# A graph layer and a gated expert network on one core: the last two gathered units are cut as 256 and 53 nodes instead of 128 and 181, and the work is listed in another order

## The chip, the core and the metric

The kernel runs on one core of one Trainium2 chip. The core's engines run beside each other and meet only at semaphores: TensorE (PE; its weight loads are shown as PEld), VectorE (DVE), ScalarE (ACT), GpSimd (POOL, which here does nothing but issue gathers) and SyncE (SP, which issues most other transfers). The metric is the device time of one execution in microseconds (us). Before the change it is 402.69 us, the median of three runs (402.5 to 402.74). All matrices are float32.

## The reference, cut to what matters

There are 3125 nodes of 256 features and 50000 edges sorted by destination.

```python
agg = jax.ops.segment_sum(features[edge_src] * edge_weight[:, None], edge_dst, num_segments=3125)
x = x + agg @ W.T + b                       # features = layernorm(x)
n = layernorm(x)
shared = mlp(n)                             # 256 -> 256 -> 128 -> 256, relu
experts = [mlp_e(n) for e in range(4)]      # 256 -> 128 -> 64 -> 256 each
gates = softmax(n @ gW + gb)                # the two best of four, weighed by softmax(top two)
x = x + shared + sum(weight_e * experts[e]) # over the two chosen
```

## The kernel before, in words

**First phase, to about 46 us.** x is loaded, normalised and multiplied by W; the products stand in SBUF (`xn_all`) and in a table in memory (`normalised_rows`). This phase isn't touched.

**Two ways to sum over edges.** Nodes 0 to 2228 are *gathered*: POOL fetches the source row of each edge by indirect DMA, 128 rows in a call and 12 calls in a batch. There are 24 batches, 0 to 23; the last has 6 calls. VectorE makes selection matrices (`selectors`, lines 1567 and 1571), TensorE multiplies them with the rows (`select_batch`, line 1154), ScalarE copies the result (`copy_windows`, line 950), and `merge` (line 1190) adds the windows of a unit up. Nodes 2229 to 3124 are *dense*: VectorE and ScalarE make one-hot matrices from edge records (`onehots`, line 1621; `low_halves`, lines 919 and 923), TensorE builds an adjacency matrix from them (`build_group`, line 1208) and multiplies it with `xn_all` (`multiply`, line 1221).

**Batches on a ring.** The rows of a batch lie in a ring of three. So before POOL fetches batch b it waits until TensorE has used batch b - 3 (line 828). Batches 0 to 2 fetch rows of x itself; their selection matrices also need the rows' statistics (`row_statistics`, lines 1518 and 1522, and `row_shifts`, line 1530).

**Units.** The nodes go through the second half (bias, residual, layer norm, gates and the expert network) as 14 units of at most two tiles of 128: G0 to G9 gathered, D0 to D3 dense. For a unit, TensorE turns the normalised rows (`turn`, line 1233), multiplies in three pieces (`layer1`, line 1253), then `layer2` (1262 and 1266), the turned gates (1275), their spread (1290) and `layer3` (1300 to 1303). ScalarE does the ReLUs (1007, 1017, 1020). VectorE does `add_bias` (1634), `residual` (1647 to 1655), `normalise` (1665), `gates` (1679), routing, `weigh` (1788) and `finish` (1796). One set of buffers serves all units, so a unit's step often waits for the unit before.

**What sets the order.** Each engine runs its list from front to back. `schedule()` makes the four lists at build time: it plays the steps with rough durations and picks by the ranks in `RANKS`, `BUILD_RANKS` and `MULT_RANKS`. `UNIT_ORDER` says in which order units open. Semaphores are waited for in the instructions themselves, so a wrong guess of `schedule()` costs a wait, in which everything behind in that engine's list stands still.

Lines that matter for what follows:

```python
# schedule(), the bias step of a unit, VectorE: for a dense unit nothing but the bias before it is asked for
("dve", "bias", 0.1 + 0.28 * T, lambda: needs(0.0 if u.kind == "D" else of("merge"), prior("bias", one)))
# add_bias, what is waited for on the chip
if q == 0:
    dve.wait_ge(s_linear, 16)
if unit.kind == "D" and unit.i == 0:
    dve.wait_ge(s_shifted, 16 * sum(stores_of(v) for v in DENSE))
# POOL, before the gathers of batch b
if b >= RING:
    pool.wait_ge(s_used[slot], b // RING)
```

`s_shifted` is counted up by the four transfers of `load_shifted` (line 762), which load x once more, laid out by the dense units' tiles. SyncE issues them behind the first edge records and the weights (lines 744 and 745).

## Time and profile before

| | |
|---|---|
| median of 3 runs | 402.69 us (402.5 to 402.74) |
| the profiled execution's own time | 399.85 us |
| its span, first to last instruction | 397.8 us |
| PE busy | 358.7 us (90%) |
| DVE busy | 278.8 us (70%) |
| ACT busy | 201.6 us (51%) |
| POOL busy | 281.3 us (71%) |
| gathers | 36 from x, 246 from the table |
| mean granted TensorE clock | 0.979 of full speed |

Times of instructions are counted from the span's start. A row of the timeline gives the start, how long the merged instructions took together, engine, line, operation, tiles written and read, and how many; in brackets stands how long the engine sat idle before it. A matmul in float32 appears as two passes (x24 for 12 matmuls). Waits are put down to whoever released them last.

### The profile page before, as it was taken

What the parts mean: (1) busy time and instruction counts of PE and PEld (TensorE: products, weight loads), DVE (VectorE), ACT (ScalarE), POOL (GpSimd) and SP (SyncE); (2) the same over time, 40 slices, a digit from 0 to 9 for tenths busy, and PEclk for the clock granted to TensorE, in tenths of its full rate; (3) what the DMA queues carried; (4) which work ended last, traced back from release to release, by engine and by line L of the source; (5) the groups of instructions that cost most, each with busy time, mean ns of one, the idle gap of its engine ahead of it and who ended that gap; (6) DMA issues with size and microseconds to landing.
All of it is one profiled execution on the core that took longest, in us unless ns stands there. A gap on an engine that the chain in (4) does not pass through costs nothing.

```text
span 397.8 us, 8069 instructions
## 1 busy us (share of the span) xinstructions
PE 358.7 (90%) x2327; PEld 283.6 (71%) x2327; DVE 278.8 (70%) x1199; ACT 201.6 (51%) x553; POOL 281.3 (71%) x294
## 2 busy tenths in 40 slices
PE   4997769969899998869999999999999999998884
PEld 3885557747687877557887877877788677766672
DVE  6698999597489999460299999770249853659671
ACT  2566797466059979300079798322019521134241
POOL 7777777777777778777777777777777777777000
PEclk9999599999999999989999999999999999999999
DMA  6999649844444463534333434343433344334000
GB/s 201 376 334 308 155 103 318 206 95 105 108 113 108 105 135 83 122 109 130 108 105 108 129 99 133 96 130 105 133 103 103 101 133 129 109 107 132 28 15 25
DMA packets 53586, 53.16 MB, mean 134 GB/s; under 512 B 32507, under 2 KB 43493, under 8 KB 53413
## 3 DMA queue, kind: packets, MB, share of 16 engines
q0 software_dynamic: 13536, 36.98, 32.1%
q1 hardware_dynamic: 35220, 10.53, 11.5%
q10 hardware_dynamic: 4784, 5.11, 3.6%
q8 instruction: 21, 0.34, 0.4%
q14 instruction: 25, 0.20, 0.2%
HBM read 46.11 MB, written 6.48 MB: 132 GB/s over the span
## 4 chain that ended last, share of the span: by engine, by line
PE 47%; SPq 30%; issue 10%; DVE 8%; DMA 2%; ACT 1%; DVEq 0%; ACTq 0%
SPq L740 23%; PE agg_ps L1221 14%; PE hid_ps L1253 10%; PE window_ps L1154 4%; PE tok_ps L1302 4%; SPq L735 4%; PE agg_ps L1190 3%; PE tok_ps L1300 2%; PE hid_ps L1266 2%; PE hid_ps L1262 2%; DVE high_node L1621 2%; SPq L734 2%; DVE gate_x L1679 1%; DMA x_sb<-in_x 1%; PE agg_ps L1208 1%
## 5 line engine op out<-in xcount | busy, mean ns | idle before, releaser
L833 POOL DMA_INDIRECT rows<-normalised_rows,src_all x246 | 243.3, 989 | 75.0 <-issue 75.0
L1221 PE MATMUL agg_ps<-xn_all,dense 128*128 128x256 f32 x350 | 84.3, 389 | 0.0
L1253 PE MATMUL hid_ps<-xt,pack 128*128 128x256 f32 (+2 forms) x336 | 70.9, 357 | 3.1 <-ACT xt L988 3.1
L1221 PEld LDWEIGHTS agg_ps<-xn_all,dense 128*128 128x128 f32 x350 | 65.3, 193 | 11.4 <-issue 3.1
L1253 PEld LDWEIGHTS hid_ps<-xt,pack 128*128 128x128 f32 x336 | 56.1, 190 | 13.7 <-issue 7.8
L919 ACT ACTIVATE low_1h<-iota,lo_f 128x128 f32<-128x128 f32 x182 | 57.6, 394 | 0.4 <-ACT xn_all L905 0.4
L1621 DVE TENSOR_SCALAR high_node<-iota,hi_f,own_w 128x125 f32<-128x125 f32 x182 | 49.8, 363 | 0.2
L1007 ACT ACTIVATE h<-hid_ps,pack 128x256 f32<-128x256 f32 (+2 forms) x84 | 32.7, 440 | 27.5 <-PE hid_ps L1253 27.3
L817 POOL DMA_INDIRECT rows<-in_x,src_first x36 | 35.6, 988 | 11.1 <-issue 10.4
L1679 DVE CUSTOM_DVE_ANT_0 gate_x<-xn,shared 128x256 f32<-128x256 f32 x100 | 41.7, 478 | 0.1
L950 ACT ACTIVATE windows<-window_ps 128x256 f32<-128x256 f32 (+1 forms) x24 | 9.1, 378 | 64.3 <-PE window_ps L1154 64.3
L1154 PE MATMUL window_ps<-rows,select 128*32 128x256 f32 x564 | 37.9, 398 | 1.5 <-DVE select L1571 1.5
L1567 DVE TENSOR_TENSOR select<-slots,rel 128x384 f32<-128x384 f32 (+1 forms) x24 | 13.1, 548 | 27.9 <-PE window_ps L1154 27.9
L1208 PE MATMUL build_ps<-high_node,low_1h 128*128 128x125 f32 x184 | 26.6, 290 | 6.7 <-ACT low_1h L923 3.5
L1208 PEld LDWEIGHTS build_ps<-high_node,low_1h 128*128 128x128 f32 x184 | 24.3, 202 | 9.9 <-issue 5.7
L923 ACT ACTIVATE low_1h<-low_1h 128x512 f32<-128x512 f32 (+1 forms) x46 | 28.8, 626 | 1.4
L1154 PEld LDWEIGHTS window_ps<-rows,select 128*32 128x32 f32 x564 | 16.7, 113 | 17.6 <-issue 7.0
L1302 PE MATMUL tok_ps<-pack,h 128*128 128x256 f32 (+1 forms) x100 | 25.7, 378 | 0.0
L1190 PE MATMUL agg_ps<-windows,place 128*128 128x256 f32 (+1 forms) x92 | 21.9, 382 | 0.3 <-ACT windows L960 0.3
L1302 PEld LDWEIGHTS tok_ps<-pack,h 128*128 128x128 f32 (+1 forms) x100 | 18.7, 187 | 3.1
L1796 DVE TENSOR_TENSOR y<-tok_ps,x 128x512 f32<-128x512 f32 (+1 forms) x14 | 8.8, 630 | 15.4 <-PE tok_ps L1303 15.3
L1190 PEld LDWEIGHTS agg_ps<-windows,place 128*128 128x128 f32 (+1 forms) x92 | 17.0, 190 | 2.9 <-issue 0.8
(171 smaller groups left out, 518.7 us busy)
## 6 DMA issues: line engine op xcount, KB each, us to landing
rows<-normalised_rows,src_all POOLq DMA_INDIRECT x246
x_sb<-in_x SPq DMA_DIRECT2D x6, 512.0 KB, 10.6
normalised_rows<-xn_all ACTq DMA_DIRECT2D x6, 512.0 KB
records<-in_rec SPq DMA_DIRECT2D x184, 1.5 KB, 1.9
out<-y SPq DMA_DIRECT2D x10, 256.0 KB
pack<-in_packed SPq DMA_DIRECT2D x1, 1540.5 KB, 9.5
dense<-in_x_cols ACTq DMA_DIRECT2D x3, 512.0 KB, 8.9
x_sb<-in_x SPq DMA_DIRECT2D x3, 256.0 KB, 10.7
```

Of the source, the lines that this page charges most:

```text
L740: sp.dma_start(records[:, bass.ds(t + (REC0[v] + t0 + k), 1), :].rearrange("p t c -> p (t c)"), rec[bass.ds(at, P), :]).then_inc(s_records ...
L817: pool.indirect_dma_start(rows[:, b * BATCH + pos, :], None, x[:, :], bass.IndirectOffsetOnAxis(ap=src_first[:, c:c + 1], axis=0)).then_in ...
L833: pool.indirect_dma_start(rows[:, b % RING * BATCH + pos, :], None, table[:, :], bass.IndirectOffsetOnAxis(ap=src_all[:, c:c + 1], axis=0) ...
L919: last = act.activation(low_1h[:, k % RING, j, :], iota[:, 0:P], ACT.Abs, scale=-1.0, bias=lo_f[:, at + j:at + j + 1])
L1154: last = pe.matmul(window_ps[SLOT * g:SLOT * (g + 1), 0:D], select[:, b % RING, j, :], rows[:, b % RING * BATCH + pos, :], start=(i == 0), ...
L1190: last = pe.matmul(sums_of(unit)[:, t * D:(t + 1) * D], place[0:full, b % KEEP, at:at + P], windows[0:full, b % KEEP, :], start=(b == batc ...
L1208: last = pe.matmul(built_in(k)[:, j * width:(j + 1) * width], low_1h[:, k % RING, j, :], high_node[:, k % RING, j, :], start=True, stop=True)
L1221: last = pe.matmul(dense_ps[0:r, t * D:(t + 1) * D], dense[:, h, t * P:t * P + r], xn_all[:, h, :], start=(h == 0 and t == 0), stop=(h == ...
L1253: last = pe.matmul(by_half(u.hid_ps[b % 2])[:, m % 2, 0:tok], w, u.xt[:, k, 0:tok], start=(k == 0), stop=(k == KD - 1))
L1302: pe.matmul(o, u.h2[:, 1 + k, c], ew3_sb[:, k, :], start=False, stop=False)
L1621: last = dve.tensor_scalar(high_node[:, r, j, :], iota[:, 0:HI * WIN], hi_f[:, at + j:at + j + 1], own_w[:, at + j:at + j + 1], ALU.is_equ ...
L1679: dve.tensor_tensor_reduce(out=gate_x[:, done % 2, :], in0=u.xn[:, t, :], in1=gate_w_sb[:, e, :], scale=1.0, scalar=gate_b_sb[:, e:e + 1], ...
```

## The change

Two things change. The last two gathered units are cut otherwise: G8 takes tiles 15 and 16 (256 nodes) and G9 only the 53 nodes of tile 17. G8's sums then need batches 19 to 22 and G9's need 22 and 23. Before, G8 needed 19 to 21, and G9, with 181 nodes, 21 to 23. And all lists are made anew with other ranks and another order of units: D0 opens ahead of G0, and D2 behind G6. No function changes.

```diff
-GATHERED += [Unit("G", 8, 15, 1, P, 15 * P), Unit("G", 9, 16, 2, P + HALF, 16 * P)]
+GATHERED += [Unit("G", 8, 15, 2, PAIR, 15 * P), Unit("G", 9, 17, 1, HALF, 17 * P)]
-UNIT_ORDER = "G0 D0 G1 G2 D1 G3 G4 G5 D2 G6 G7 G8 D3 G9"
+UNIT_ORDER = "D0 G0 G1 G2 D1 G3 G4 G5 G6 D2 G7 D3 G8 G9"
-RANKS = {"open": 3, "near": 0.07, "behind": 0.36, "dve_behind": 0.94, "act_behind": 0.23, "hurry": 1.58,
+RANKS = {"open": 3, "near": 0.06, "behind": 0.27, "dve_behind": 0.42, "act_behind": 0.23, "hurry": 1.58,
...
-MULT_RANKS = (1.55, 1.41, 10.13, 3.23)
+MULT_RANKS = (1.27, 1.41, 9.18, 3.23)
```

VectorE's list where the first phase ends. Line 1579 is the last step ahead of the lists, 1825 the branch into them, 1621 the one-hots of groups 2 and 3, 1587 and 1589 the first records of block 1. What an instruction waits for stands in brackets. Before:

```order
L1579 TENSOR_SCALAR place<-iota,posn 128x256 [waits s_posn]
L1825 TENSOR_LOAD flag
L1825 ISA x2
L1825 COMPARE_AND_BRANCH
L1621 TENSOR_SCALAR high_node<-iota,hi_f,own_w 128x125 [waits s_keys]
L1621 TENSOR_SCALAR high_node<-iota,hi_f,own_w 128x125 x3
L1621 TENSOR_SCALAR high_node<-iota,hi_f,own_w 128x125 [waits s_keys,s_built]
L1621 TENSOR_SCALAR high_node<-iota,hi_f,own_w 128x125 x3
L1587 TENSOR_SCALAR hi_i<-records 128x16 [waits s_records1]
```

The same place now:

```order
L1579 TENSOR_SCALAR place<-iota,posn 128x256 [waits s_posn]
L1825 TENSOR_LOAD flag
L1825 ISA x2
L1825 COMPARE_AND_BRANCH
L1634 TENSOR_TENSOR x_sb<-x_sb,shared 128x512 [waits s_shifted,s_x_turned,s_linear]
L1621 TENSOR_SCALAR high_node<-iota,hi_f,own_w 128x125 [waits s_keys]
L1621 TENSOR_SCALAR high_node<-iota,hi_f,own_w 128x125 x3
L1621 TENSOR_SCALAR high_node<-iota,hi_f,own_w 128x125 [waits s_keys,s_built]
L1621 TENSOR_SCALAR high_node<-iota,hi_f,own_w 128x125 x3
L1587 TENSOR_SCALAR hi_i<-records 128x16 [waits s_records1]
```

The bias of D0 (line 1634, 128x512) has moved from far behind to the head of the list.

VectorE from there to the selection matrices of batch 1 (1567 and 1571), before. 1518 and 1522 are the statistics of batch 1's rows:

```order
L1608 SCALAR_TENSOR_TENSOR own_w<-own_w,records 128x16
L1518 BN_STATS row_stats<-rows 128x6 x12
L1522 BN_AGGR row_mv<-row_stats 128x2 x12
L1621 TENSOR_SCALAR high_node<-iota,hi_f,own_w 128x125 x8
L1530 TENSOR_TENSOR row_w<-w_all,row_rstd 128x12
L1621 TENSOR_SCALAR high_node<-iota,hi_f,own_w 128x125 x4
L1567 TENSOR_TENSOR select<-slots,rel 128x384
L1571 TENSOR_TENSOR select<-select,row_w 128x384
```

Now:

```order
L1608 SCALAR_TENSOR_TENSOR own_w<-own_w,records 128x16
L1518 BN_STATS row_stats<-rows 128x6 x12
L1522 BN_AGGR row_mv<-row_stats 128x2 x12
L1621 TENSOR_SCALAR high_node<-iota,hi_f,own_w 128x125 x4
L1530 TENSOR_TENSOR row_w<-w_all,row_rstd 128x12
L1621 TENSOR_SCALAR high_node<-iota,hi_f,own_w 128x125 x4
L1567 TENSOR_TENSOR select<-slots,rel 128x384
L1571 TENSOR_TENSOR select<-select,row_w 128x384
```

One group of four one-hots has moved behind them.

TensorE's list around the last two batches (1154; x12 is batch 22, x6 is batch 23). Before, where 128x128 at line 1253 is D3 and the last three rows belong to D3 and G9:

```order
L1253 MATMUL hid_ps<-xt,pack 128x128 x4
L1154 MATMUL window_ps<-rows,select 32x256 x6
L1253 MATMUL hid_ps<-xt,pack 128x128 x4
L1190 MATMUL agg_ps<-windows,place 128x256 x4
L1253 MATMUL hid_ps<-xt,pack 128x128 x4
L1262 MATMUL hid_ps<-h,pack 128x128 x2
L1266 MATMUL hid_ps<-h,pack 64x128 x4
L1275 MATMUL mid_ps<-ident_b,parts 79x128
L1290 MATMUL tok_ps<-mix_t,owner 128x128 x2
L1233 MATMUL mid_ps<-ident,xn 128x128 x4
```

Now, where the x5 at line 1190 is the merge of G8, the x4 at line 1233 its turn, the 128x256 at line 1253 its first layer and the x2 at line 1190 the merge of G9:

```order
L1154 MATMUL window_ps<-rows,select 32x256 x12
L1253 MATMUL hid_ps<-xt,pack 128x128 x4
L1190 MATMUL agg_ps<-windows,place 128x256 x5
L1253 MATMUL hid_ps<-xt,pack 128x128 x4
L1262 MATMUL hid_ps<-h,pack 128x128 x2
L1266 MATMUL hid_ps<-h,pack 64x128 x4
L1275 MATMUL mid_ps<-ident_b,parts 79x128
L1154 MATMUL window_ps<-rows,select 32x256 x6
L1290 MATMUL tok_ps<-mix_t,owner 128x128 x2
L1233 MATMUL mid_ps<-ident,xn 128x128 x4
```

A whole unit of 256 nodes (G8) now stands behind batch 22, with its turn behind batch 23, and the 53 nodes of G9 come last. GpSimd's list is the same.

## Rows read from the trace of the kernel before

**Rows 1.** The page: busy time and share of the span.

```profile
PE 358.7 (90%) x2327; PEld 283.6 (71%) x2327; DVE 278.8 (70%) x1199; ACT 201.6 (51%) x553; POOL 281.3 (71%) x294
```

**Rows 2.** What POOL waited for: engine, line, releaser, us, times, longest.

```profile
POOL rows L833 <- issue: 75.0, 246, 0.3
```

**Rows 3.** Timeline of POOL: first gathers of batches 3, 4; last of 22, 23.

```profile
50.13 0.95 POOL L833 DMA_INDIRECT rows<-normalised_rows,src_all  x1 [0.30 <-issue]
...
65.56 0.95 POOL L833 DMA_INDIRECT rows<-normalised_rows,src_all  x1 [0.30 <-issue]
...
359.32 1.15 POOL L833 DMA_INDIRECT rows<-normalised_rows,src_all  x1 [0.30 <-issue]
...
367.12 0.95 POOL L833 DMA_INDIRECT rows<-normalised_rows,src_all  x1 [0.30 <-issue]
```

**Rows 4.** Stretches: span, POOL busy, clock, DMA share, GB/s.

```profile
70.00:72.00 2.00, 1.54 (x2) 1.00 1.08 342
72.00:74.00 2.00, 1.55 (x2) 1.00 1.23 255
...
76.00:78.00 2.00, 1.41 (x2) 1.00 0.40 77
```

**Rows 5.** The four transfers of line 762: first and last start, time to landing.

```profile
L762 SPq DMA_DIRECT2D x_sb<-in_x x4: 434/570/679, 60.7 to 62.6; - x4
DMA to landing us min/median/max: 10.5/10.8/11.3
```

**Rows 6.** Timeline of VectorE after the first phase.

```profile
46.26 2.36 DVE L1621 TENSOR_SCALAR high_node<-iota,hi_f,own_w 128x125 f32<-128x125 f32 x8
...
56.51 1.10 DVE L1621 TENSOR_SCALAR high_node<-iota,hi_f,own_w 128x125 f32<-128x125 f32 x4
...
58.11 0.56 DVE L1571 TENSOR_TENSOR select<-select,row_w 128x384 f32<-128x384 f32 x1
...
87.02 0.68 DVE L1634 TENSOR_TENSOR x_sb<-x_sb,shared 128x512 f32<-128x512 f32 x1
```

**Rows 7.** TensorE: batches 0, 1, 22 (line 1154) and sixteen products (line 1221).

```profile
45.85 2.79 PE L1154 MATMUL window_ps<-rows,select 128*32 128x256 f32 x24 [1.50 <-DVE select L1571]
...
59.26 1.50 PE L1154 MATMUL window_ps<-rows,select 128*32 128x256 f32 x24
...
61.69 7.08 PE L1221 MATMUL agg_ps<-xn_all,dense 128*128 128x256 f32 x32
...
363.80 1.50 PE L1154 MATMUL window_ps<-rows,select 128*32 128x256 f32 x24
```

**Rows 8.** What ended VectorE's and TensorE's two longest waits near 170 us.

```profile
DVE hi_i L1587 <- DMA records<-in_rec: 8.7, 3, 4.8
...
PE tok_ps L1290 <- DVE mix_t L1781: 7.1, 5, 4.6
```

**Rows 9.** A stretch after the last gather: span, TensorE busy, clock, DMA share, GB/s.

```profile
370.00:371.00 1.00, 1.00 (x8) 1.00 0.00 0
```

**Rows 10.** TensorE and PEld near the end: G7, G8, D3, and the last output.

```profile
343.96 0.60 PE L1233 MATMUL mid_ps<-ident,xn 128*128 128x128 f32 x4
...
356.93 0.70 PE L1300 MATMUL tok_ps<-pack,h 128*128 128x256 f32 x2 [0.85 <-DVE h L1788]
...
359.74 0.27 PE L1303 MATMUL tok_ps<-b_parts,mix_t 79*128 79x256 bf16 x1
...
360.77 2.90 PEld L1253 LDWEIGHTS hid_ps<-xt,pack 128*128 128x128 f32 x24 [0.78 <-issue]
360.80 3.07 PE L1253 MATMUL hid_ps<-xt,pack 128*128 128x128 f32 x24 [0.57 <-ACT xt L988]
...
375.99 1.16 PE L1253 MATMUL hid_ps<-xt,pack 128*128 128x128 f32 x8
...
382.09 0.27 PE L1303 MATMUL tok_ps<-b_parts,mix_t 79*128 79x256 bf16 x1
...
393.44 0.69 DVE L1796 TENSOR_TENSOR y<-tok_ps,x 128x512 f32<-128x512 f32 x1 [3.32 <-PE tok_ps L1303]
```

More of the change, by code:

```diff
@@ L165 @@
 STATS_BEHIND = 3
-UNIT_ORDER = "G0 D0 G1 G2 D1 G3 G4 G5 D2 G6 G7 G8 D3 G9"
-RANKS = {"open": 3, "near": 0.07, "behind": 0.36, "dve_behind": 0.94, "act_behind": 0.23, "hurry": 1.58,
-         "batch": 0.99, "rawturn": 1.65, "rawlin": -10.68, "merge": 1.53, "windows": 4.07,
-         "built": 1.89, "rowstd": 2.86, "rawxt": 6.45, "rawout": -0.2, "low": 7.97, "select": -3.77,
-         "select_late": 8.67, "place": 7.59, "records": 6.65, "onehot": 0.5, "rowstats": 3.06,
-         "rowshifts": -1.63}
-BUILD_RANKS = (3.27, 4.1, 2.6, -3.72)
-MULT_RANKS = (1.55, 1.41, 10.13, 3.23)
+UNIT_ORDER = "D0 G0 G1 G2 D1 G3 G4 G5 G6 D2 G7 D3 G8 G9"
+RANKS = {"open": 3, "near": 0.06, "behind": 0.27, "dve_behind": 0.42, "act_behind": 0.23, "hurry": 1.58,
+         "batch": 0.99, "rawturn": 1.36, "rawlin": -10.4, "merge": 1.53, "windows": 4.07, "built": -3.9,
+         "rowstd": 2.86, "rawxt": 6.06, "rawout": 0.18, "low": 7.76, "select": -4.24,
+         "select_late": 7.28, "place": 5.89, "records": 3.37, "onehot": 0.5, "rowstats": 3.46,
+         "rowshifts": -2.1}
+BUILD_RANKS = (3.02, 4.36, 6.09, -3.72)
+MULT_RANKS = (1.27, 1.41, 9.18, 3.23)
 GATHER_US = 1.275
```

## The prediction

> **What bounds the kernel now.** I read the page first: TensorE is busy 90% of the span, everything else far less [rows 1]. That looks like a TensorE kernel, so the next view is the waits of POOL, the one engine with a fixed amount of work that nothing can hide: its 246 gathers from the table never waited for another engine, only for their own issue, 0.3 us each [rows 2]. Its timeline says what that means: from 50.13 to the last gather at 367.12 there are 246 gathers, so (367.12 - 50.13) / 245 = 1.29 us each, 15.5 us for a batch of 12, without a gap [rows 3]. The last nodes can't be summed before the last rows are there. The transfers end within the 2.9 us from 367.12 to 370.0 [rows 3, 9]; I take 2.7 us from issue to landing, so batch 22's rows land at 359.32 + 2.7 = 362.0 and batch 23's at 369.8. TensorE reaches batch 22 at 363.80 [rows 7], 1.8 us later. So POOL and TensorE are nearly even: a stop of POOL's stream lengthens the kernel by nearly its whole length, and a few us won on TensorE alone bring little.
>
> **Part one: D0's bias at the head of VectorE's list.** For the planner the step is free at once. On the chip it waits for `s_shifted`, four transfers that SyncE issues at 60.7 to 62.6 and that land 10.5 to 11.3 us later [rows 5], the last at 62.6 + 11.3 = 73.9. Before, the step stood at 87.02 and waited for nothing [rows 6]. VectorE begins its list at 46.26 [rows 6], so now it stands still there for some 25 us, and with it everything behind: the one-hots of groups 2 and 3 (TensorE's builds, and ScalarE's `low_halves` two groups later), the records, the statistics of batch 1's rows and batch 1's selection matrices. TensorE does its builds 0 and 1 and batch 0, and then waits as well.
>
> POOL isn't stopped at once. It fetches batch 3, and before batch 4 it needs batch 1 used. Before, TensorE began batch 1 at 59.26 [rows 7] and POOL went on at 65.56 [rows 3]: 6 us to spare, no more. The new time is a sum:
> - Landing. While the four transfers run, the DMA engines are full (shares 1.08 and 1.23 from 70 to 74, against 0.40 once only gathers are left) [rows 4]. POOL now falls silent after 66.8, which frees 0.4 of the engines for up to 9 us, 3.7 us of their time. I take 2.4 us off: 71.5. Bounds: 73.9 as traced, and 70 if all of it goes to these transfers.
> - The bias itself, 0.68 us [rows 6]: 72.2.
> - From the first one-hot to batch 1's selection matrices it took 58.11 + 0.56 - 46.26 = 12.4 us; one group of one-hots, 1.05 us, has moved behind: 11.3 us [rows 6]. Hence 83.5.
> - TensorE uses the first third of batch 1. At full clock that is 1.50 / 3 = 0.5 us, and after an idle time, as for batch 0, 2.79 / 3 = 0.9 us [rows 7]. With the semaphores 0.7 us: 84.2.
>
> POOL is held from 65.56 to 84.2: **18.6 us** (17 to 21 by the bounds).
>
> **Can it be held again, or catch up?** It can't catch up: the gathers have a fixed pace. Batch 5 needs batch 2 used. Behind batch 1's matrices VectorE now has five groups of one-hots (5.3), records and statistics (6.0: what 46.26 to 56.51 holds beside sixteen one-hots [rows 6]), a small block of records and three short steps (2.8): 14.1 us. TensorE has batch 1, 22 products of two passes at 7.08 / 32 = 0.22 us [rows 7], so 9.7, two builds and two steps on raw rows, about 14 us in all. POOL comes back to the ring after 15.5 + 0.7 us. That leaves about 2 us, so I count nothing, and up to 3 us for the range. Later batches have more room, since TensorE's lag is no larger than POOL's and shrinks: near 170 us it waited 4.6 us for VectorE, which itself stood 4.8 us on records from SyncE [rows 8]. SyncE's stream runs on by itself, so 18 us later these records are there (D3's last block, whose step has moved ahead of G1's `weigh`, would otherwise have cost some 10 us). The two waits are covered by the hold and bring nothing, because POOL sets the pace.
>
> **Part two: the cut of the last units.** Counted from batch 22's landing, the last output was made at 393.44 + 0.69 = 394.1, or 32.1 us [rows 10]. Now TensorE is there in time and waits for the rows. Behind batch 22 come D3's remaining layers and G8's merge, all done before batch 23's rows at 7.8 us, and batch 23 stands ahead of G8's turn: 7.8 + 1.5 + 0.3 = 9.6 us. For a unit of 256 nodes the trace has G7, from its turn at 343.96 to its third layer at 356.93, 13.0 us with batch 21 in it [rows 10]. G8 has no batch in it (-1.5), but G9's merge (+1.0), D3's third layer, half of it uncovered (+0.7), G9's turn and a third of its first layer (+1.2): 14.4 us, so G8's third layer begins at 24.0. It takes 359.74 + 0.27 - 356.93 = 3.1 us for two tiles [rows 10]: 27.1. G9's other two thirds of the first layer: 2.0, so 29.1. From there D3 needed 382.09 + 0.27 - (375.99 + 1.16) = 5.2 us to the end of its third layer [rows 10]; G9 has narrower ReLUs and no other unit between, 4.8: 33.9. Its output step, 0.5: 34.4 against 32.1. The stores took 397.8 - 394.1 = 3.7 us; two small ones, 3.5. In sum 34.4 + 3.5 - 32.1 - 3.7 = 2.1; I take **+2.0 us** (0 to +5): the 53 nodes are a unit of their own behind a full one, and the full one can't begin before batch 23.
>
> For the narrow passes I used the width of 128, since weight loads don't shrink: 24 loads take 2.90 us and the passes 3.07 us at 128 columns [rows 10], 121 ns a load. If the passes went by columns alone, the 16 behind G8 would take 16 x 53 ns = 0.9 us instead of 2.0, and the sum would be 1.1 us less. The Trainium skill, TensorE: Matmul & The Clock Gate, section on LDWEIGHTS, says that a load takes the time of its stationary columns over 1.2 GHz, whatever is moved past it. That would be an estimate of 107 ns for 128 columns, 1.7 us for the 16; it speaks against splitting off 53 nodes, and the row agrees in kind and is a little higher.
>
> **The sum.** 18.6 + 2.0 = 20.6 us on the profiled execution's 399.85 us (span 397.8): 420.5, span 418.4. The runs' median is 402.69, 2.84 above the profiled execution, so the measured time should be 402.69 + 20.6 = **423.3 us**, 5.1% slower. Not counted is the clock: it stood at half for batch 0, the engine's first work in the lists after an idle time, 2.79 us instead of 1.50 [rows 7]. Before batch 22 TensorE will idle again for some us, and could run the next few at half speed, 0 to 2 us more.
>
> **The rivals.**
> 1. *TensorE becomes the bound.* After the hold its whole backlog lies in front of it. By my count it reaches batch 22 some 3 us ahead of the rows; if the first part costs it 5 us more (half clock and sparse one-hots from 72 to 100), it comes 2 to 5 us late and everything ends there. For it: 90% busy. Against: it had idle time in the first 100 us which the hold swallows. 426 to 428 us. Chance 0.12.
> 2. *The ring jams again.* Batch 2 comes 3 us later than I think, POOL stands before batch 5 too, and the same before 6. For it: a margin of only 2 us. Price 3 to 8 us: 427 to 432. Chance 0.09.
> 3. *A shorter hold.* The transfers land at 67 to 69, since POOL is silent: the hold is 14 to 16 us, 418 to 421. Against: the engines are already full before POOL stops, and 10.5 us was the shortest landing. Chance 0.07.
> 4. *The other side: no hold, and the cut pays.* If the transfers were there when VectorE asks, POOL would never stop, and G9 with one tile could run right behind batch 23, in gaps that TensorE finds in G8. From batch 23's landing at 369.8: batch and merge 2, residual, norm and turn 4, first layer 3.1, ReLU 0.6, then 4.8 and 0.5: 15 us, so 384.8 instead of 394.1. It decides at a landing before 52 us, when the slack of 6 us would swallow the wait; the issue at 60.7 [rows 5] excludes that, unless the four aren't what the step waits for. 393 to 396 us. Chance 0.03; and 0.01 for nothing at all, at 402.7.
>
> **How the numbers follow.** My case has 0.68 and its own range is 420 to 427. Rivals 1 and 2 reach to 432, rival 3 to 418. With 2 in 10 left out: 418 to 430. This kernel can be told from no change at about 0.2%, 0.8 us; faster than that has 0.03, within it 0.01, slower 0.96.
>
> **What would show it right or wrong.** In the changed kernel's profile: line 1634, 128x512, as VectorE's first step after line 1579, at about 71.5 with some 25 us idle before it, released by a transfer; batch 1 at about 83.5; POOL's 13th table gather at about 84.2 with a wait of 18 to 19 us on TensorE, the only one of its kind; the last gather near 385.7; TensorE waiting for rows at batch 22 or 23; no long wait on records. The last output some 34 us after batch 22's rows. Wrong it is if VectorE doesn't wait there, if POOL is held under 14 or over 22 us, or if the end moves other than POOL's last gather by more than 5 us.

## The result, and the profile after

The changed kernel takes **424.54 us** (median of 4 runs, 423.46 to 424.84), the kernel before 402.72 on the same terms (4 runs, 402.5 to 403.1). The ratio is 1.055, with a 95% interval of 1.0508 to 1.0591: it is slower by about 22 us, where 423.3 was forecast. An execution now and then falls into a slower state; ratios leave such executions out, medians don't. The profiled execution took 424.84, its span is 422.8.

The page of the changed kernel: busy time, then three lines of the 40 slices (10.6 us each).

```profile
PE 362.3 (86%) x2327; PEld 288.0 (68%) x2327; DVE 278.7 (66%) x1199; ACT 203.5 (48%) x553; POOL 277.1 (66%) x294
...
PE   5996300699798789999999899999999999999985
...
POOL 7777771057777777777777777777777777773000
PEclk9997655699899988999999999999999999999997
```

The busy times are those of before within 5 us [rows 1]; the span grew by 25.0. So most of the added time is not work but idle time, and the slices show where: TensorE at 3, 0, 0 in slices 5 to 7, POOL at 1 and 0 in slices 7 and 8. The line of the clock falls with it.

Waits of POOL and TensorE in the changed kernel (engine, line, releaser, us, times, longest):

```profile
POOL rows L833 <- PE window_ps L1154: 21.8, 1, 21.8
```
```profile
PE build_ps L1208 <- DVE high_node L1621: 30.8, 3, 26.9
```

Before, POOL had no wait for TensorE [rows 2]. The releaser named is TensorE, which itself waited 26.9 us for VectorE. The chain is complete only with VectorE's timeline:

```profile
44.85 0.42 DVE L1579 TENSOR_SCALAR place<-iota,posn 128x256 f32<-128x256 f32 x1
72.87 0.69 DVE L1634 TENSOR_TENSOR x_sb<-x_sb,shared 128x512 f32<-128x512 f32 x1 [27.60 <-DMA x_sb<-in_x]
73.48 2.12 DVE L1621 TENSOR_SCALAR high_node<-iota,hi_f,own_w 128x125 f32<-128x125 f32 x8
...
84.12 0.56 DVE L1571 TENSOR_TENSOR select<-select,row_w 128x384 f32<-128x384 f32 x1
```

The bias of D0 is the first step of the list and waits 27.60 us for a transfer [rows 6 for its old place]. The four transfers and their landing:

```profile
L762 SPq DMA_DIRECT2D x_sb<-in_x x4: 434/510/924, 60.8 to 62.8; - x4
...
DMA to landing us min/median/max: 9.9/10.0/10.2
```

62.8 + 10.0 = 72.8: the landing is the end of the wait. (The times from issue to landing are 9.9 to 10.2 us; VectorE starts at 72.87.) Next TensorE, and then POOL, of the changed kernel:

```profile
44.98 2.79 PE L1154 MATMUL window_ps<-rows,select 128*32 128x256 f32 x24 [2.01 <-DVE select L1571]
74.64 2.07 PE L1208 MATMUL build_ps<-high_node,low_1h 128*128 128x125 f32 x8 [26.86 <-DVE high_node L1621]
...
82.57 2.07 PE L1208 MATMUL build_ps<-high_node,low_1h 128*128 128x125 f32 x8 [1.63 <-DVE high_node L1621]
84.44 1.71 PE L1208 MATMUL hid_ps<-high_node,low_1h 128*128 128x125 f32 x8
86.08 1.50 PE L1154 MATMUL window_ps<-rows,select 128*32 128x256 f32 x24
...
385.22 1.50 PE L1154 MATMUL window_ps<-rows,select 128*32 128x256 f32 x24
```
```profile
64.25 0.95 POOL L833 DMA_INDIRECT rows<-normalised_rows,src_all  x1 [0.30 <-issue]
87.02 0.95 POOL L833 DMA_INDIRECT rows<-normalised_rows,src_all  x1 [21.82 <-PE window_ps L1154]
...
377.03 0.95 POOL L833 DMA_INDIRECT rows<-normalised_rows,src_all  x1 [0.30 <-issue]
...
384.55 0.95 POOL L833 DMA_INDIRECT rows<-normalised_rows,src_all  x1 [0.30 <-issue]
```

Without the hold POOL's next gather would start at 64.25 + 0.95 + 0.30 = 65.50, as before at 65.56 [rows 3]. It starts at 87.02, 21.5 later. The last gather is only 17.4 later (384.55 against 367.12): the gathers won back 4 us. Batch 22 begins 21.4 later (385.22 against 363.80 [rows 7]).

Stretches of the changed kernel: from-to, length, busy time (instructions) of TensorE, PEld, DVE, ACT, POOL, then the granted clock, DMA share, GB/s.

```profile
44.00:100.00 56.00, 25.55 (x152) 20.68 (x152) 27.36 (x126) 23.53 (x63) 26.25 (x28) 0.69 0.47 123
100.00:385.20 285.20, 272.72 (x1809) 217.28 (x1808) 194.34 (x815) 143.15 (x390) 217.22 (x224) 0.98 0.42 113
385.20:419.00 33.80, 29.88 (x195) 21.73 (x194) 21.80 (x105) 12.04 (x41) 0.30 (x1) 0.97 0.09 28
...
350.00:380.00 30.00, 30.00 (x187) 23.16 (x186) 13.38 (x53) 8.73 (x23) 22.83 (x24) 1.00 0.40 116
...
416.00:420.00 4.00, 2.84 (x9) 1.13 (x8) 0.69 (x2) 0.19 (x1) 0.00 (x0) 0.61 0.03 8
```

And the same three stretches of the kernel before, up to its own batch 22 and its last output:

```profile
44.00:100.00 56.00, 46.79 (x338) 35.36 (x337) 48.02 (x213) 40.50 (x114) 43.15 (x43) 0.92 0.62 160
100.00:363.80 263.80, 252.43 (x1647) 201.19 (x1647) 176.69 (x740) 126.68 (x348) 201.39 (x205) 0.99 0.42 113
363.80:394.00 30.20, 24.46 (x173) 17.63 (x172) 19.23 (x93) 10.38 (x35) 3.35 (x4) 1.00 0.11 34
```

From 44 us to batch 22 TensorE has 298.3 us of work after and 299.2 before, the same. Its idle time grew from 20.6 to 42.9 us. The wait at the head is 26.9 of these, so the rest shrank by 4.6: that is all that TensorE made good. In the 30 us from 350 to 380 it is busy for all 30.00, and POOL gathers at its own pace. Batch 22's rows were there at 377.03 + 2.7 = 379.7, TensorE came at 385.22. The 2.7 us from issue to landing are the prediction's estimate; in experiment 6, where TensorE waits for batch 22's rows, it is 380.31 - 377.41 = 2.9. So the rows came 17.7 us later than before, TensorE 21.4, and TensorE set the end.

The last output and the stores of the changed kernel:

```profile
419.31 0.42 DVE L1796 TENSOR_TENSOR y<-tok_ps,x 128x256 f32<-128x256 f32 x1 [2.81 <-PE tok_ps L1303]
```

From batch 22's start to the end of that it is 419.73 - 385.22 = 34.5 us, against 394.13 - 363.80 = 30.3 before [rows 7, 10]. The span's sum: 21.4 (batch 22 begins later) + 4.2 (from there to the last output) - 0.6 (stores, 3.1 against 3.7) = 25.0.

### The profile page after: what moved, and what is told of

It is laid out like the page before. It is cut to its first block, busy times and chain, and to the rows that moved or that the text cites. A ratio compares the mean times of both kernels' runs of the same rounds, so it can differ in the third digit from the quotient of the medians.

```text
span 422.8 us, 8068 instructions
## 1 busy us (share of the span) xinstructions
PE 362.3 (86%) x2327; PEld 288.0 (68%) x2327; DVE 278.7 (66%) x1199; ACT 203.5 (48%) x553; POOL 277.1 (66%) x294
## 3 DMA queue, kind: packets, MB, share of 16 engines
q0 software_dynamic: 13536, 36.98, 30.3%
q1 hardware_dynamic: 35204, 10.53, 10.4%
## 4 chain that ended last, share of the span: by engine, by line
PE 63%; DVE 12%; SPq 12%; issue 5%; ACT 4%; DMA 2%; DVEq 0%
PE agg_ps L1221 18%; PE hid_ps L1253 12%; SPq L740 6%; PE window_ps L1154 6%; PE tok_ps L1302 6%; PE agg_ps L1190 4%; PE build_ps L1208 3%; PE tok_ps L1300 3%; PE hid_ps L1262 3%; PE hid_ps L1266 3%; DVE gate_x L1679 3%; DVE high_node L1621 2%; DMA x_sb<-in_x 2%; PE agg_ps L1208 2%; SPq L728 1%
## 5 line engine op out<-in xcount | busy, mean ns | idle before, releaser
L833 POOL DMA_INDIRECT rows<-normalised_rows,src_all x246 | 238.8, 971 | 96.5 <-issue 74.7
L1221 PE MATMUL agg_ps<-xn_all,dense 128*128 128x256 f32 x350 | 82.5, 382 | 0.9 <-ACT dense L969 0.9
L1253 PE MATMUL hid_ps<-xt,pack 128*128 128x256 f32 (+2 forms) x336 | 72.1, 359 | 1.0 <-ACT xt L988 1.0
L1253 PEld LDWEIGHTS hid_ps<-xt,pack 128*128 128x128 f32 x336 | 57.3, 190 | 10.6 <-issue 3.2
L1208 PE MATMUL build_ps<-high_node,low_1h 128*128 128x125 f32 x184 | 29.3, 310 | 35.5 <-DVE high_node L1621 30.8
L1208 PEld LDWEIGHTS build_ps<-high_node,low_1h 128*128 128x128 f32 x184 | 26.5, 219 | 38.9 <-DVE high_node L1621 36.9
L817 POOL DMA_INDIRECT rows<-in_x,src_first x36 | 35.9, 996 | 11.1 <-issue 10.4
L1302 PE MATMUL tok_ps<-pack,h 128*128 128x256 f32 (+1 forms) x100 | 27.7, 401 | 0.0
L1634 DVE TENSOR_TENSOR x_sb<-x_sb,shared 128x512 f32<-128x512 f32 (+1 forms) x14 | 8.8, 626 | 27.6 <-DMA x_sb<-in_x 27.6
L1302 PEld LDWEIGHTS tok_ps<-pack,h 128*128 128x128 f32 (+1 forms) x100 | 19.7, 197 | 3.7 <-issue 0.6
L1647 DVE TENSOR_TENSOR x<-agg_ps,x_sb 128x512 f32<-128x512 f32 (+1 forms) x14 | 8.8, 629 | 19.3 <-PE agg_ps L1221 18.8
## 6 DMA issues: line engine op xcount, KB each, us to landing
dense<-in_x_cols ACTq DMA_DIRECT2D x3, 512.0 KB, 10.2
```

Source lines behind the costliest of these rows:

```text
L817: pool.indirect_dma_start(rows[:, b * BATCH + pos, :], None, x[:, :], bass.IndirectOffsetOnAxis(ap=src_first[:, c:c + 1], axis=0)).then_in ...
L833: pool.indirect_dma_start(rows[:, b % RING * BATCH + pos, :], None, table[:, :], bass.IndirectOffsetOnAxis(ap=src_all[:, c:c + 1], axis=0) ...
L1208: last = pe.matmul(built_in(k)[:, j * width:(j + 1) * width], low_1h[:, k % RING, j, :], high_node[:, k % RING, j, :], start=True, stop=True)
L1221: last = pe.matmul(dense_ps[0:r, t * D:(t + 1) * D], dense[:, h, t * P:t * P + r], xn_all[:, h, :], start=(h == 0 and t == 0), stop=(h == ...
L1253: last = pe.matmul(by_half(u.hid_ps[b % 2])[:, m % 2, 0:tok], w, u.xt[:, k, 0:tok], start=(k == 0), stop=(k == KD - 1))
L1302: pe.matmul(o, u.h2[:, 1 + k, c], ew3_sb[:, k, :], start=False, stop=False)
```

## Experiments

Ratios are to the kernel before, run beside each experiment on the same chip, with their 95% intervals. Experiments 1 to 4 ran on one chip, 5 to 8 and 12 on a second, 9 to 11 on a third. The runs of the kernel before spread over 398 to 408 us, more than the 0.2% that I gave as the resolution (one more, beside experiment 12, took 1088.97 us; it is in no ratio). Differences of 1 to 2 us are read with that in mind, above all where two experiments of different chips are compared.

**1. D0's bias moved behind, in the changed kernel.** Its place in VectorE's list alone is changed, to just ahead of the first gathered unit's bias.

```diff
+_d = ORDER["dve"]
+_bias = next(i for i in _d if i[0] == "bias" and i[1] == DENSE[0])
+_d.remove(_bias)
+_d.insert(next(n for n, i in enumerate(_d) if i[0] == "bias"), _bias)
```

> The changed kernel with one step moved: D0's bias goes from the head of VectorE's list to just ahead of G0's bias; cut and order are otherwise the new ones. Hold theory (the wait of that step for the four transfers costs nearly all): POOL's 13th table gather starts near 65.5 us without a wait, and the time falls by 15 to 21 us from 424.5, to 404 to 409 (the new cut's end costs 2 to 4 us, and a wait on records near 165 us, which the hold had covered, may cost TensorE up to 10 us, of which the rows' arrival hides a part). Rival (the new cut and the rest of the new order cost most of it): 415 or more.

Measured: 402.77 us (10 runs), ratio 1.0027 (0.9988 to 1.0066). POOL has no wait for TensorE left, and its last gather starts at 363.53:

```profile
POOL rows L838 <- issue: 75.0, 246, 0.3
```

One step's place was the whole 22 us, within the noise. The time is below the 404 to 409 that I expected: I had given the new cut's end 2 to 4 us. What is left of the rest of the change, the new order and the cut together, can't be told from zero.

**2. The same fault put into the kernel before.** The biases of G0 and D0 go to the head of its VectorE list.

```diff
+_d = ORDER["dve"]
+_two = [i for i in _d if i[0] == "bias"][:2]
+_d[:] = _two + [i for i in _d if i not in _two]
```

> The kernel before with the first two bias steps (G0's and D0's) moved to the head of VectorE's list, cut and order otherwise the old ones. Hold theory: VectorE stands until 73 us, POOL is held about 21 us before batch 4, the time is 418 to 425. Rival (cut and order are the cause): under 410.

Measured: 420.69 us (4 runs), ratio 1.048 (1.0411 to 1.055). Its waits:

```profile
POOL rows L837 <- PE window_ps L1158: 25.0, 1, 25.0
...
DVE x_sb L1638 <- DMA shared<-in_every: 20.7, 1, 20.7
...
DVE x_sb L1638 <- DMA x_sb<-in_x: 7.3, 1, 7.3
```

As expected (418 to 425). The hold needs neither the new cut nor the new order. VectorE waits twice here: G0's bias for `shared`, a transfer that the prediction had not named, and behind it D0's bias for the shifted tiles, until 74.59. The hold is 25.0 us and not the 21 that I expected.

**3. The cut alone**, with the ranks and the order of before.

```diff
-GATHERED += [Unit("G", 8, 15, 1, P, 15 * P), Unit("G", 9, 16, 2, P + HALF, 16 * P)]
+GATHERED += [Unit("G", 8, 15, 2, PAIR, 15 * P), Unit("G", 9, 17, 1, HALF, 17 * P)]
```

> The kernel before with the new cut (G8 256 nodes, G9 53) and the old order of units and ranks, so that the planner makes the lists from these. No hold: POOL's last gather near 367. All of G8, D3 and G9 now stands behind batch 23. Hold theory: the cut costs only at the end, 2 to 9 us, 405 to 412. Rival that the cut is the cause of the slowdown: 418 or more. Rival that the cut pays by itself: under 402.

Measured: 410.8 us (4 runs), ratio 1.0212 (1.0113 to 1.0311), within the 405 to 412 expected. TensorE's timeline at batches 22 and 23:

```profile
361.63 2.79 PE L1154 MATMUL window_ps<-rows,select 128*32 128x256 f32 x24 [4.52 <-DMA rows<-normalised_rows,src_all]
...
368.67 1.49 PE L1154 MATMUL window_ps<-rows,select 128*32 128x256 f32 x12 [1.33 <-DMA rows<-normalised_rows,src_all]
```

Here TensorE runs dry ahead of the last rows, since the list keeps D3, G8 and G9 all for behind them: it has 33.9 us of work behind batch 22 in place of 24.5. The first batch after the wait runs at a granted clock of 0.50 (2.79 in place of 1.50). So in the order of before the new cut costs 1 to 3%.

**4. The order alone**, with the cut of before.

```diff
-GATHERED += [Unit("G", 8, 15, 2, PAIR, 15 * P), Unit("G", 9, 17, 1, HALF, 17 * P)]
+GATHERED += [Unit("G", 8, 15, 1, P, 15 * P), Unit("G", 9, 16, 2, P + HALF, 16 * P)]
```

> The changed kernel with the old cut (G8 128 nodes, G9 181): the new order of units and ranks alone. Hold theory: D0's bias is still at the head of VectorE's list, so POOL is held about 21 us and the time is 419 to 425. Rival (the cut is the cause): under 410. What it is less than 424.5 is what the new cut costs in the new order; I expect 1 to 4 us.

Measured: 428.06 us (4 runs), ratio 1.0653 (1.058 to 1.0727). A miss: I held that the cut costs something, and took it off; without it the kernel is 3.5 us slower. POOL's hold is 24.1 us here, 2.3 longer than with the cut. Experiment 11 tries to separate the two.

**5. The shifted tiles loaded earlier**, with the bias at the head of the list as changed.

```diff
...
             sp.wait_ge(s_table, 16 * len(groups))
+            load_shifted()
             for i in range(2, FORE):
                 load_records(i)
             load_weights()
-            load_shifted()
```

> The changed kernel, lists untouched, with SyncE's four transfers of line 762 issued right after its wait for the table, ahead of blocks 2 and 3 of the records and of the weights. D0's bias still stands at the head of VectorE's list. Hold theory: the transfers start near 40 us and land near 50 us, VectorE stands some 5 us instead of 27.6, batch 1 is used before POOL asks (slack of some 6 us), POOL isn't held, and the time is that of the kernel with the bias moved, 401 to 405. Rival (the place of the bias in the list costs in another way than by this landing): 415 or more.

Measured: 417.65 us (4 runs), ratio 1.0385 (1.0345 to 1.0426). A miss by 13 us, and the most useful one. VectorE and POOL:

```profile
66.49 0.69 DVE L1634 TENSOR_TENSOR x_sb<-x_sb,shared 128x512 f32<-128x512 f32 x1 [22.14 <-DMA shared<-in_every]
```
```profile
81.21 0.95 POOL L833 DMA_INDIRECT rows<-normalised_rows,src_all  x1 [15.67 <-PE window_ps L1154]
```

The first bias of the list has a second transfer to wait for, `shared`, by way of `s_linear`. It is issued at 61.8, lands at 66.4, and had been hidden behind the shifted tiles (in the changed kernel: issued at 60.0, landed 4.7 us later, against 72.8). Taking one wait away uncovered the next, which ends 6.4 us earlier, and the hold shrank by 6.1.

**6. Less work for TensorE**: 12 of the 25 source tiles of D2's product left out, so D2's sums are incomplete.

```diff
-                for t in tiles:
+                for t in tiles if not (v == 2 and 8 <= h < 20) else ():
```

> The changed kernel with 12 of the 25 products of D2 left out (source tiles 8 to 19, so D2's sums are incomplete): 24 matmuls of 0.43 us, 10.4 us less for TensorE between 330 and 350 us. In the changed kernel batch 22 was used at 385.2, its last rows were issued at 377.0. TensorE bound at the end: the time falls by some 5 us, until batch 22 waits for its rows near 379.7, so 418.5 to 420.5. POOL's rows bound (as I predicted): no change, 424 to 425. TensorE alone bound: 10 us less, 414.

Measured: 420.28 us (4 runs), ratio 1.0445 (1.0396 to 1.0495). The hold is still there (22.7 us), but with 10.4 us less to do TensorE waits for rows at batches 19 and 22:

```profile
335.07 1.50 PE L1154 MATMUL window_ps<-rows,select 128*32 128x256 f32 x24 [2.42 <-DMA rows<-normalised_rows,src_all]
...
380.31 1.50 PE L1154 MATMUL window_ps<-rows,select 128*32 128x256 f32 x24 [0.85 <-DMA rows<-normalised_rows,src_all]
```

Of the 10.4 us only 4.3 shorten the kernel, and batch 22 comes 4.9 earlier; then the rows bind. That is what I expected for TensorE as the bound at the end (418.5 to 420.5), and not for my own case (424 to 425). So in the changed kernel TensorE's backlog set the end, 5 us behind the rows.

**7. TensorE kept busy in the last unit**: four products without use, into a free bank, on the kernel of experiment 1.

```diff
+            def filler(q):
+                if q == len(UNITS) - 1:
+                    pe.matmul(window_ps[:, 0:D], sw2_sb[:, 0, :], gnn_wt_sb[:, 0, :], start=True, stop=True)
...
+                        filler(q)
                         layer2(q)
```

and in the same way ahead of the turned gates, the spread and the third layer.

> The kernel with the bias moved, and four matmuls of 0.43 us into an unused bank put into TensorE's list ahead of G9's layer 2, turned gates, spread and layer 3, where it waits for ReLUs and VectorE. If the half clock at the end (0.50 from 396 us) comes from TensorE's idle time between G9's narrow steps, the clock stays full, G9's third layer takes 1.4 instead of 2.7 us and the time falls by about 1 us, to 401 to 402.5. Rival (fillers only stand in the way, or the clock falls anyway): 403 to 404.5.

Measured: 402.92 us (12 runs), ratio 0.9976 (0.9933 to 1.0018); experiment 1's was 1.0027 on another chip. The median lies between my range (401 to 402.5) and the rival's (403 to 404.5), so the time decides nothing; the trace does. The end of experiment 1, and then that of the filled kernel:

```profile
395.47 1.91 PE L1307 MATMUL tok_ps<-pack,h 128*53 128x256 f32 x4
...
396.00:400.00 4.00, 1.59 (x5) 0.49 (x3) 0.42 (x1) 0.00 (x0) 0.00 (x0) 0.50 0.08 21
```
```profile
394.85 1.03 PE L1307 MATMUL tok_ps<-pack,h 128*53 128x256 f32 x4
...
392.00:396.00 4.00, 3.99 (x27) 2.39 (x26) 0.45 (x2) 0.70 (x3) 0.00 (x0) 1.00 0.02 6
```

The last layer runs at 1.00 in place of 0.50: 0.88 us less for its four products of line 1307. So the clock falls there in the narrow work with idle time between, and stays when that time is filled; the gain in time is too small to be seen alone.

**8. The last block of records later**, behind G2's finish, on the kernel of experiment 1.

```diff
+_rec = next(i for i in _d if i[0] == "records" and i[1] == len(BLOCKS) - 1)
+_d.remove(_rec)
+_d.insert(next(n for n, i in enumerate(_d) if i[0] == "finish" and i[1] == GATHERED[2]) + 1, _rec)
```

> The kernel with the bias moved, and VectorE's step on the last block of records moved from ahead of G1's weigh to behind G2's finish. In the kernel with the bias moved VectorE stood 3.0 us on it at 169.4 and TensorE 2.75 us behind. If TensorE bounds the end, the time falls by 1.5 to 3 us, to 400 to 401.5, and batch 22 comes that much earlier. Rival (POOL's rows bound, or the wait moves on to another step): within 0.8 us of 402.8.

Measured: 401.58 us (12 runs), ratio 0.9977 (0.995 to 1.0005). In experiment 1 the block was waited for, and TensorE with it (VectorE's row, then TensorE's):

```profile
169.43 0.17 DVE L1592 TENSOR_SCALAR hi_i<-records 128x12 int32<-128x12 int32 x1 [2.98 <-DMA records<-in_rec]
```
```profile
171.22 0.70 PE L1305 MATMUL tok_ps<-pack,h 128*128 128x256 f32 x2 [2.75 <-DVE h L1793]
```

Both are gone here. The time is 1.2 us below experiment 1's, where I expected 1.5 to 3, and batch 22 begins at 362.49 in place of 363.54. That is no more than the noise between the two chips, so the gain isn't shown by this run alone.

**9. Both loads early**, `shared` and the shifted tiles, after experiment 5: the bias still at the head.

```diff
-                sp.dma_start(shared[:, :], every.to_broadcast([P, D + E * D + E])).then_inc(s_linear, 16)
...
             sp.wait_ge(s_table, 16 * len(groups))
+            sp.dma_start(shared[:, :], every.to_broadcast([P, D + E * D + E])).then_inc(s_linear, 16)
+            load_shifted()
             for i in range(2, FORE):
                 load_records(i)
             load_weights()
-            load_shifted()
```

> The changed kernel with both loads that D0's bias waits for, `shared` and the shifted tiles, issued right behind the table's wait, ahead of record blocks 2 and 3; VectorE's list is the changed one, D0's bias still at its head. Theory (the hold follows the later of the two landings): with only the shifted tiles early the wait ended at 66.5 us by `shared`, the hold was 15.7 us and the last gather stood at 379.1. With both issued at 44 to 47 us they land at 50 to 58, select.1 follows 11 to 12 us behind, at 62 to 70, so GpSimd waits 0 to 6 us, the last gather is at 364 to 370 and the time 402 to 408. Rival (it is something else in the new lists, not the landing): GpSimd waits over 12 us once more and the time stays at 415 or above.

Measured: 405.32 us (7 runs), ratio 1.0108 (1.0076 to 1.014), as expected.

```profile
53.77 0.69 DVE L1634 TENSOR_TENSOR x_sb<-x_sb,shared 128x512 f32<-128x512 f32 x1 [7.10 <-DMA x_sb<-in_x]
```
```profile
68.15 0.94 POOL L833 DMA_INDIRECT rows<-normalised_rows,src_all  x1 [2.33 <-PE window_ps L1154]
```

With the changed kernel and experiment 5 that makes three points of one line: VectorE starts at 53.77, 66.49, 72.87, POOL is held 2.3, 15.7, 21.8 us. Carried on, the line puts the end of the hold at a landing near 51 us. Experiment 4, with the old cut, lies about 1 us above it (VectorE starts at 74.28, POOL is held 24.1).

**10. All that helped, together**: experiments 1, 7 and 8 in one kernel.

> D0's bias behind the first gathered unit's, the last record block's step behind G2's finish, and the four filler products of TensorE in the last unit, all three together on the changed kernel. Theory: each alone gave 402.8, 401.6 and 402.9; TensorE's stall near 170 us (2.75) is gone and the third layer of the last unit runs at full clock (about 1.5 us less), which makes 399.5 to 401.5 and a ratio of 0.993 to 0.998 to the kernel before. Rival: the end hangs on the gathers' pace, which differs from run to run by more than either, and the time is 401.5 to 403.

Measured: 399.8 us (12 runs, 397.58 to 405.55), the kernel before 401.95 (26 runs), ratio 0.9946 (0.991 to 0.9982). It is within the 399.5 to 401.5 expected and faster than both kernels, by 0.5% of before and, by the two ratios, 5.7% of the changed one. Which of the three parts brings how much can't be told. Its profiled execution happened to be its longest, so only its clock is read: 1.00 in every stretch from 384 us to the end.

**11. The order without the hold, with the old cut**: experiment 1 with the cut line of experiment 4.

> The new order with the old cut of the last two units (one tile, and 181 nodes), and D0's bias just ahead of the first gathered unit's, so that the hold does not arise. It differs from the kernel with the bias moved alone (402.8) only in the cut. With the hold in place the old cut was 3.5 us slower than the new one (428.06 to 424.54), and its hold 2.3 us longer. Theory (most of the 3.5 was the longer hold): the cut is worth 0 to 1.5 us, and this comes to 402.5 to 404.5. Rival (the new cut has less behind the last batch's rows, in the order made for it): 405 to 407.

Measured: 404.59 us (12 runs), ratio 1.0087 (1.0057 to 1.0117), between my two ranges (the theory's ends at 404.5). Against experiment 1 (1.0027) the new cut is worth about 0.6%, 2 us, in the order made for it. Of the 3.5 us of experiment 4 something over 1 is then the longer hold. From batch 22 to the end of TensorE's last step it is 362.47 to 399.28, 36.8 us, where experiment 1 has 34.1. The two kernels ran on different chips, so the 2 us is uncertain by about as much, and how the 3.5 us divide isn't settled. What is clear is that the cut's worth hangs on the order: in the order of before it costs 2% (experiment 3).

**12. The slow gather of the kernel before.** Its trace has one gather of 3.13 us; those of experiments 2 and 3, where the same VectorE steps follow each other, have one of 3.13 and 4.06 beside them; no trace with the new lists has one over 1.45. The kernel before, and with it an unbroken row of VectorE steps from 147.37 (D1's bias, the copy of `mix_t`, eight gates, `weigh`) to the one-hots at 152.02:

```profile
149.19 3.13 POOL L833 DMA_INDIRECT rows<-normalised_rows,src_all  x1 [0.30 <-issue]
```

```diff
+_d = ORDER["dve"]
+_b = [i for i in _d if i[0] == "bias"][4]
+_d.remove(_b)
+_d.insert(next(n for n, i in enumerate(_d) if i[0] == "weigh" and i[1] == GATHERED[1]) + 2, _b)
```

> The kernel before with the bias of D1 (VectorE, 147.37 us) moved behind the eight gate products, `weigh` of G1 and one step of one-hots; nothing else. In all three traces with the order of before one gather takes 3.13 to 4.06 us (at 149.19, 174.16 and 146.29) and ends 0.3 us after the start of the first one-hots behind an unbroken row of VectorE steps: bias, copy of mix_t, eight gates, weigh; no trace with the new order has one over 1.5. Theory (that row of steps holds GpSimd's gather): without the bias at its front the slow gather is gone, none is over 1.6 us, line 833's busy time falls from 243.3 to 240 or 241, and the last gather starts 2 us earlier, near 365; the time falls by 0 to 2 us. Rival (the gates alone hold it, whatever stands ahead): one gather of 3 to 4 us stays near 149 and the time is that of before within 0.8 us.

Measured: 401.16 us (12 runs), the kernel before 402.09 (17 runs), ratio 0.9983 (0.9945 to 1.0021). The slow gather is gone, the longest takes 1.36, and the gathers are busy for 239.1 us in place of 243.3, as in the changed kernel (238.8). The last one starts at 361.83, 5.3 earlier: 4.2 by the gathers' busy time, of which the one slow gather is 2.2, and 1.1 because their stream began earlier (49.03 against 50.13). The time can't be told from that of before: batch 22's rows are there at 354.33 + 2.7 = 357.0, 5.0 us earlier than before, and TensorE begins it at 367.30, 3.5 later than before. So earlier rows alone bring nothing in this kernel either. Shown is that the slow gather stands in all three traces that have this step ahead of the gates, and is gone in the one that has it elsewhere; which of the steps in the row holds it is left open.

## Why the prediction was right

The cause, its place and most of its size were right. The account of the end was not, by the prediction's own sign: it called itself wrong if the end moved other than POOL's last gather by more than 5 us, and the span's end moved by 25.0, the last gather by 17.4. That the times agree within 1.3 us is in part luck, as the sum below shows.

**The mechanism and its place were right.** D0's bias waits at the head of VectorE's list for the transfers issued at 60.8; POOL is held once, and it is the only long hold. Experiments 1, 2, 5 and 9 show it by removing it, by making it in the other kernel and by moving the landing.

**The landing** was taken at 71.5, with 70 to 73.9 as bounds; it came at 72.8. I had taken 2.4 us off the longest time to landing, 11.3, since POOL falls silent; the longest was 10.2, 1.1 less, and the median 10.0 in place of 10.8. That POOL's silence is what brought this isn't shown.

**Bias to selection matrices**: 72.2 to 83.5 forecast, 11.3 us; measured 73.56 to 84.68, 11.1.

**TensorE to the first third of batch 1** was put at 0.7 us and took 2.3 (84.68 to 87.02). This term failed. Two builds stand ahead of the batch, and I counted them as done. They waited for their one-hots until 82.57 and ran at a mean granted clock of 0.60 and 0.55 in the two stretches from 82 to 86 us (2.07 and 1.71, where the next two, at 87.51 and 88.50, take 1.16 and 1.06), so TensorE came to batch 1 at 86.08, 1.4 us after its matrices. So POOL was held for 21.5 us against 18.6: 1.4 more by the landing, 1.6 by this term, 0.2 less between them. It is just above the bound of 21 that I gave.

**"Can't catch up" was wrong in part.** I took the pace of the gathers as fixed. After the hold it was (384.55 - 87.02) / 233 = 1.277 us, where before it was (367.12 - 65.56) / 233 = 1.294 [rows 3]: 4.0 us over the 233 intervals. 2.2 of them are the one gather of 3.13 of before, which experiment 12 traces to the old list of VectorE and which no trace with the new order has. The other 1.8 are many gathers a little shorter, for which I have no cause. I had read the mean of the pace and not its largest value.

**The end: rival 1, not my case.** I had TensorE reach batch 22 some 3 us ahead of the rows and gave the other 0.12. It came 5.5 us behind them, and experiment 6 gives 5. What failed is the sentence that TensorE is there in time, since it had idle time which the hold would swallow. The stretches show what there was: 20.6 us idle from 44 to 363.8, of which only 4.6 went against a stall of 26.9. On the spans the end came 4.4 us behind my case, inside the 3 to 5 us that rival 1 adds to it; its own range, 426 to 428, was missed for the reason under the sum. The rows came at 379.7, earlier than the 380.6 forecast: the longer hold (2.9) and the faster gathers (4.0) nearly cancel.

**No second hold, no long wait on records**: right. The wait in front of D3's last block near 170 us is covered by the hold, as said, and comes back with experiment 1.

**The tail.** From batch 22's start to the last output I had 34.4 us, and 34.5 were measured. In part this is luck. My first term, 9.6 us to G8's turn, waited for batch 23's rows; these were there at 384.55 + 2.7 = 387.3, and it was TensorE's own work that took 9.3 us. G9's first layer ended at 28.6 in place of 29.1. From there to the end of its third layer I had 4.8 us and 5.4 were measured: the narrow passes were sized rightly, but the third layer ran at a lower clock, which the sum did not have (TensorE, then the weight loads of the first row):

```profile
411.94 1.89 PE L1253 MATMUL hid_ps<-xt,pack 128*128 128x53 f32 x16
...
416.56 0.79 PE L1300 MATMUL tok_ps<-pack,h 128*53 128x256 f32 x2 [0.43 <-DVE h L1788]
417.14 1.91 PE L1302 MATMUL tok_ps<-pack,h 128*53 128x256 f32 x4
418.85 0.42 PE L1303 MATMUL tok_ps<-b_parts,mix_t 79*53 79x256 bf16 x1
```
```profile
411.83 1.86 PEld L1253 LDWEIGHTS hid_ps<-xt,pack 128*128 128x128 f32 x16
```

The passes of 53 columns take 1.89 / 16 = 118 ns each, at a granted clock of 1.00, their weight loads 1.86 / 16 = 116, and passes of 128 columns 3.07 / 24 = 128 [rows 10]: the width hardly counts, the weight load binds. The Trainium skill, TensorE: Matmul & The Clock Gate, section on LDWEIGHTS, has a load take its columns over 1.2 GHz, which makes 107 ns for 128 columns, an estimate; the passes of the trace are 10% above it. The four passes of line 1302 take 1.03 in place of 1.91 at full clock, those of line 1300 0.64 in place of 0.79 and line 1303's 0.27 in place of 0.42 (experiment 7): 1.2 us are lost. I had 0 to 2 us for the clock beside the sum, but in front of batch 22, where TensorE didn't idle.

**The sum.** On the span 422.8 stands against 418.4. By my own steps batch 22 was to begin at 363.8 + 18.6 - 1.8 = 380.6 and began at 385.22, 4.6 us later; the rest is as forecast (34.5 for 34.4, stores 3.1 for 3.5). The rows themselves came 0.9 earlier than forecast, so all of the miss is TensorE's backlog. The medians differ by 21.8 and not by 25.0, because the profiled execution of before was 2.9 us faster than its median and that of the changed kernel 0.3 slower. On the profiled executions the forecast, 420.5, misses 424.84 by 4.3 us; on the medians 423.3 misses 424.54 by 1.2. The difference is luck.

**Rivals 2, 3 and 4** did not come. Rival 4's rule fits as far as it was tried: at a landing of 53.8 the hold is 2.3, which points to an end near 51.5, where I had said 52 (a slack of 6 us). Its price was not. Without the hold the cut and the order bring no 393 to 396 but 402.8 (experiment 1): TensorE comes last there too. Batch 22 begins at 363.54, where its rows were there 5 us earlier (355.89 + 2.7 = 358.6), and behind it the new kernel has 30.2 us of TensorE's work, where the kernel before has 24.5.

## What to carry to other kernels

A step's place in an in-order list must be held against when its data land, all of them: look for every semaphore it waits for, not the last one in the trace, since removing that only shows the next. Put nothing at the head of a list that waits for a bulk transfer, when a short step behind it feeds a ring with 6 us to spare. And before saying who catches up, take each engine's busy time and idle time from the stall to the end: TensorE, busy for 272.7 of the 285.2 us that were left (96%), could not make the stall good.

## What the runs showed of the hardware that I had not expected

- After the 26.9 us of idle time TensorE's granted clock was at 0.50 for the first builds, at 1.00 from 80 to 82 us, and fell again, though TensorE was busy for 0.94 of 2 us there and for 1.43 and 2.00 in the next two stretches. Stretches of the changed kernel:

```profile
76.00:78.00 2.00, 2.00 (x12) 2.00 (x11) 1.86 (x9) 1.80 (x5) 0.00 (x0) 0.50 0.10 6
...
80.00:82.00 2.00, 0.94 (x4) 0.48 (x3) 1.97 (x17) 1.94 (x7) 0.00 (x0) 1.00 0.08 2
82.00:84.00 2.00, 1.43 (x6) 1.43 (x7) 2.00 (x9) 1.97 (x7) 0.00 (x0) 0.60 0.14 3
84.00:86.00 2.00, 2.00 (x11) 1.96 (x10) 1.97 (x8) 1.53 (x5) 0.00 (x0) 0.55 0.07 2
```

So the work behind a stall can run slower for some us as well: the two builds ahead of batch 1 took 1.6 us more than the two behind it.

- At the end the clock falls to 0.5 though TensorE is busy 2.70 of 4 us (experiment 1, 392 to 396, 0.90, and 0.50 behind it). With four products without use (0.65 to 0.70 us each) between, it stayed at 1.00 (experiment 7).
- A gather of GpSimd took 3.13 to 4.06 us in place of 0.95 beside one unbroken row of VectorE steps, and 1.03 at most beside it once a step was taken out of the row's front (experiment 12). The Trainium skill, SBUF — State Buffer, section "SBUF: two separate sides", says that GpSimd can't write the descriptors of its transfers while VectorE runs an operation in a two-port mode on the port pair that both share. That fits in kind, but no run here tells whether any of these steps is such an operation; the same eight gates stand beside gathers of 1.19 us at most elsewhere in the trace of before.
- The runs of one kernel differ by several us (experiment 10: 397.6 to 402.8, and one of 405.6); what makes that difference is left open.
